# Turning tiles on TensorE in the type of the rounded halves, through second names over the same bytes

## What is computed

```python
x = x + xattn(layernorm(x), ctx, ctx, mask, wq, wk, wv, wo)   # x, ctx: (8, 512, 512)
x = x + ffn(layernorm(x), Wr, Wg, Wu, Wd, Sg, Su, Sd, expert_bias)

# xattn: H = 16 heads of 32, KVH = 2 heads of K and V
scores = einsum('bhqd,bhkd->bhqk', rope(Q), rope(K)) / sqrt(32)
out = einsum('bhqk,bhkd->bhqd', softmax(where(mask == 0, -1e9, scores)), V) @ wo
# ffn: 8 experts of width 256, two per token, beside a shared one of width 512
h = silu(gate) * up
out = sum over the two experts of weight * (h @ Wd) + silu(xf @ Sg) * (xf @ Su) @ Sd
```

## Time and profile before

| | |
|---|---|
| time of three runs, us | 1424.04, 1426.14, 1426.20; median 1426.14 |
| span of the profiled execution, us | 1422.9 (it has no other time of its own) |
| TensorE busy | 1373.1 us (97%) |
| weight loads (PEld) busy | 1067.2 us (75%) |
| VectorE busy | 960.4 us (67%) |
| ScalarE busy | 844.9 us (59%) |
| GpSimd busy | 581.4 us (41%) |
| chain that ended last | TensorE 82%, VectorE 6%, ScalarE 4% |

### The profile page before, as it was taken

The page is one execution under the profiler, slowest core; times in us unless marked ns, Lnnn a source line. Parts: engine busy times, 40 slices in busy tenths (PEclk is TensorE's granted clock), DMA queues, the critical chain, the costliest instruction groups (busy, mean ns, idle before and its releaser), DMA issues.

```text
span 1422.9 us, 28293 instructions
## 1 busy us (share of the span) xinstructions
PE 1373.1 (97%) x8110; PEld 1067.2 (75%) x8110; DVE 960.4 (67%) x2655; ACT 844.9 (59%) x1951; POOL 581.4 (41%) x724
## 2 busy tenths in 40 slices
PE   6898999999999999999898999999999999999997
PEld 4675777877777777777576777777777888888885
DVE  6888888888888888988777666666653334333342
ACT  2788979889798897988983222222213434444342
POOL 4443523435244343342253432333334555555553
PEclk9899999999999999999999999999999999999999
DMA  5545464564645646445465222222257779785542
GB/s 203 152 145 146 135 190 139 152 185 137 188 136 149 187 131 190 142 140 157 114 202 203 85 87 90 82 75 84 73 140 205 201 178 260 204 197 103 111 76 37
DMA packets 146070, 206.62 MB, mean 145 GB/s; under 512 B 35456, under 2 KB 73088, under 8 KB 145923
## 3 DMA queue, kind: packets, MB, share of 16 engines
q1 hardware_dynamic: 124562, 166.91, 38.1%
q0 software_dynamic: 17952, 33.64, 12.3%
q10 hardware_dynamic: 3408, 4.26, 0.9%
HBM read 105.49 MB, written 69.35 MB: 123 GB/s over the span
## 4 chain that ended last, share of the span: by engine, by line
PE 82%; DVE 6%; ACT 4%; issue 3%; DMA 2%; SPq 1%; POOL 1%; DVEq 0%; POOLq 0%; ACTq 0%
PE psum L693 13%; PE psum L1494 13%; PE psum L1496 12%; PE psum L1495 12%; PE psum L808 7%; PE psum L787 7%; PE psum L738 3%; PE psum L739 3%; PE psum L740 3%; ACT a_probs L591 2%; PE psum L1561 2%; PE psum L708 2%; DVE a_probs L955 1%; ACT a_probsT L597 1%; PE psum L1590 1%
## 5 line engine op out<-in xcount | busy, mean ns | idle before, releaser
L591 ACT ACTIVATE a_probs<-a_probs,a_low 128x512 f32<-128x512 f32 x512 | 366.6, 716 | 83.7 <-DVE a_low L955 82.2
L955 DVE CUSTOM_DVE_ANT_0 a_probs<-psum,a_bias 128x512 f32<-128x512 f32 x512 | 345.4, 685 | 76.5 <-PE psum L787 73.2
L693 PE MATMUL psum<-a_ident,a_probs 128*128 128x128 f32 x2048 | 311.0, 274 | 7.8 <-ACT a_probsT L597 5.9
L693 PEld LDWEIGHTS psum<-a_ident,a_probs 128*128 128x128 f32 x2048 | 245.3, 141 | 77.0 <-issue 25.6
L787 PE MATMUL psum<-a_kT,a_q_stack 128*128 128x512 f32 x512 | 247.2, 484 | 10.1 <-DVE a_low L955 5.4
L597 ACT ACTIVATE a_probsT<-psum 128x512 f32<-128x512 f32 x328 | 190.7, 582 | 10.0 <-PE psum L693 10.0
L1363 POOL DMA_INDIRECT out<-b_y,b_pairs_sb x71 | 112.6, 1586 | 148.7 <-DMA out<-b_y,b_pairs_sb 85.9
L1795 DVE SCALAR_TENSOR_TENSOR b_v_hidden<-b_v_hidden,psum 128x256 f32<-128x256 f32 x71 | 29.9, 421 | 165.9 <-ACT b_v_hidden L1459 165.9
L961 DVE COPY a_probsT<-psum 128x512 f32<-128x512 f32 x184 | 126.0, 685 | 6.1 <-PE psum L693 4.2
L1494 PE MATMUL psum<-b_w,b_vT_hi 128*128 x284 | 117.4, 413 | 0.1
L808 PE MATMUL psum<-a_probsT,a_v 128*32 128x512 f32 x1024 | 116.7, 595 | 0.0
(11 more groups left out here) (218 smaller groups left out, 3054.3 us busy)
## 6 DMA issues: line engine op xcount, KB each, us to landing
b_w<-w_halves SPq DMA_DIRECT2D x16, 1536.0 KB
a_q_stack<-a_qT_hi SPq DMA_DIRECT2D x254, 64.0 KB, 2.0
a_q_stack<-a_qT_lo SPq DMA_DIRECT2D x253, 64.0 KB, 2.0
w_halves<-a_w_hi SPq DMA_DIRECT2D x96, 128.0 KB, 2.0
w_halves<-a_w_lo SPq DMA_DIRECT2D x96, 128.0 KB, 1.9
a_xT_in<-in_x_turned SPq DMA_DIRECT2D x32, 256.0 KB, 2.9
a_ctx_in<-in_ctx SPq DMA_DIRECT2D x32, 256.0 KB, 3.0
a_x_in<-in_x SPq DMA_DIRECT2D x32, 256.0 KB, 3.2
```

The source lines that it names most:

```text
L591: nc.scalar.activation(probs[:, h % 2, t], probs[:, h % 2, t], ACT.Exp, bias=low[:, h % H, t:t + 1], scale=-1.0, accum_out=total[:, h // G ...
L693: last = nc.tensor.transpose(out[:, P * i:P * (i + 1)], src(i), identity[:])
L955: nc.vector.tensor_tensor_reduce(probs[:, h % 2, t], psum[:, t % 2], bias[:, t], 1.0, HUGE, ALU.add, ALU.min, low[:, h % H, t:t + 1]).then ...
```

## The change

The turns of probabilities, Q, normalised rows, gathered rows and hidden tiles are asked for in `F32R`. For each of those tiles a second tensor is allocated over the same bytes with the type `F32R` (`bits`), the output in PSUM is named in that type by `bitcast`, and the moving operand is `ident_r`. The two identities swap their places in memory, so that `ident_r` is the one that stays through the feed-forward. Each engine has as many instructions as before, in the same order.

```diff
-    "rope_q": 94208, "rope_k": 95232, "ident_r": 96256, "pick_raw": 96768, "pick": 97280, "probsT": 98304, "bias": 139264, "kT": 147456,
+    "rope_q": 94208, "rope_k": 95232, "ident_r": 207872, "pick_raw": 96768, "pick": 97280, "probsT": 98304, "bias": 139264, "kT": 147456,
...
-    "wkv": 205824, "ident": 207872, "k_cos": 208384, "k_sin": 208640, "k_rot": 208896, "low": 209152, "total": 209408, "inverse": 209664,
+    "wkv": 205824, "ident": 96256, "k_cos": 208384, "k_sin": 208640, "k_rot": 208896, "low": 209152, "total": 209408, "inverse": 209664,
...
+    def bits(name, shape):
+
+        return nc.alloc_sbuf_tensor_at(f"a_{name}_bits", shape, F32R, offset=base + ATTENTION_PLACES[name])
...
+    probs_bits = bits("probs", [P, 2, TT, L])
+    q_bits = bits("q", [P, 2, TT, D])
...
-        def four(out, src, identity):
+        def four(out, src):
             for i in range(4):
-                last = nc.tensor.transpose(out[:, P * i:P * (i + 1)], src(i), identity[:])
+                last = nc.tensor.transpose(out[:, P * i:P * (i + 1)].bitcast(F32R), src(i), ident_r[:])
             return last
...
-            four(in_ring(part, b, "qT", i), lambda t: q[:, batch, t, P * g:P * (g + 1)], ident).then_inc(s["qT_filled"], 1)
+            four(in_ring(part, b, "qT", i), lambda t: q_bits[:, batch, t, P * g:P * (g + 1)]).then_inc(s["qT_filled"], 1)
...
-            four(out, lambda c: probs[:, h % 2, t, P * c:P * (c + 1)], ident).then_inc(s["t_filled"], 1)
+            four(out, lambda c: probs_bits[:, h % 2, t, P * c:P * (c + 1)]).then_inc(s["t_filled"], 1)
...
+    xn_bits, rows_bits, v_hidden_bits = bits("xn", [P, XN_SLOTS, D]), bits("rows", [P, X_SLOTS, D]), bits("v_hidden", [P, 2, F])
...
-                last = nc.tensor.transpose(psum[:, XT + n % 2, P * c:P * (c + 1)], xn[:, n % XN_SLOTS, P * c:P * (c + 1)], ident[:])
+                last = nc.tensor.transpose(psum[:, XT + n % 2, P * c:P * (c + 1)].bitcast(F32R), xn_bits[:, n % XN_SLOTS, P * c:P * (c + 1)], ident_r[:])
...
-                last = nc.tensor.transpose(psum[:, XT + n % 2, P * c:P * (c + 1)], rows[:, n % X_SLOTS, P * c:P * (c + 1)], ident[:])
+                last = nc.tensor.transpose(psum[:, XT + n % 2, P * c:P * (c + 1)].bitcast(F32R), rows_bits[:, n % X_SLOTS, P * c:P * (c + 1)], ident_r[:])
...
-                mm = nc.tensor.transpose(psum[:, HT + n % 2, P * i:P * (i + 1)], v_hidden[:, n % 2, i:F:FC], ident[:])
+                mm = nc.tensor.transpose(psum[:, HT + n % 2, P * i:P * (i + 1)].bitcast(F32R), v_hidden_bits[:, n % 2, i:F:FC], ident_r[:])
```

More of the change, by code:

```diff
@@ L1076, in on_vector @@
         bodies(dve, body)
-    shared = dict(s, ident=ident, half=half, stored=stored, stacked=stacked)
+    shared = dict(s, ident_r=ident_r, half=half, stored=stored, stacked=stacked)
     return shared, on_sync, on_gpsimd, on_scalar, on_tensor, on_vector
 def ffn_phase(nc, ctx, psum, attention, k, x2_rows, xn_rows, out_rows, xn_all, out_all, wr, sg, su, sd, expert_bias, pairs, halves, tile_table):
+    tile_at = {}
     where = [(nc.sbuf_base + 31) // 32 * 32]
@@ L1092, in put, with bits @@
             where[0] = (at + size + 31) // 32 * 32
+        tile_at[name] = at
         return nc.alloc_sbuf_tensor_at("b_" + name, shape, dt, offset=at)
+    def bits(name, shape):
+        return nc.alloc_sbuf_tensor_at(f"b_{name}_bits", shape, F32R, offset=tile_at[name])
     def sem(name):
@@ L1121, in ffn_phase @@
     pairs_sb = put("pairs_sb", [P, VISITS, 2], I32)
-    ident, half = attention["ident"], attention["half"]
+    ident_r, half = attention["ident_r"], attention["half"]
     tri, ones = put("tri", [P, P], at=constants), put("ones", [P, P], at=constants + 512)
```

## The result

The changed kernel takes 1415.06 us (median of 4 runs, 1409.39 to 1415.83), the kernel before 1426.02 on the same chip (4 runs). The ratio is 0.9918, with a 95% interval of 0.9900 to 0.9936. That is 11 us less, where 36 were forecast, and 10 us above the top of the range. The profiled execution has a span of 1414.0 us, 8.9 less than before, and a mean granted clock of 0.985 (before 0.994).

A forecast was written before the change was run, and what follows sets the result against it. TensorE was taken to bound every stage, with VectorE and ScalarE close behind in the attention. 29 us there plus 7 in the feed-forward made 36, from 1426.1 to 1390 us; range 1350 to 1405 us.

The forecast's parts named there:

- What a rounded turn costs: All rounded turns: the load sets the pace at 0.085 us against 0.109, saving 0.07 us a group of four.
- The first rival: All rounded turns: the load hides as well, a turn costs 0.06 us, kernel at 1351 us; chance 0.17.
- the second, that nothing changes: All rounded turns: loads go at the ordinary 0.11 us or the type has no effect, 1426 us; chance 0.08.
- I take the middle of 21 and 38, 29 us: Attention: gain between 21 us, limited by other engines' idle time, and 38 us, with TensorE the bound everywhere.
- its own sign of being wrong: Attention: the prediction is wrong if this gives less than 21 us though turns have the forecast pace.
- The least of 2.6 us a batch: Attention: eight windows' gains, each capped by idle time of the busier of VectorE and ScalarE; 21 us over eight batches.
- The reason for going above the least: Attention: four banks and six steps of scores let TensorE run ahead and spend its lead later; up to 38 us.
- The low end of the range, 1376 us: Whole kernel: fastest end of the forecast, from turn distances of 0.08 to 0.09 and 21 to 38 us for the attention.
- third rival: Attention: shorter passes make TensorE look idle, the clock drops to half, kernel ends slower at 1442 us; chance 0.05.
- What is late next: Attention: once turns are shorter, ScalarE's exp and VectorE's add and minimum are late; no size given.
- 103 x 0.07 = 7 us: Feed-forward: groups of normalised and gathered rows each gain 0.07 us, all of it on the path.
- I count 0, with 0 and 71 x 0.07 = 5 us as ends: Expert visits: the 71 pairs of hidden tiles gain nothing, as their load sets the pace already; at most 5 us.

The follow-up runs named there:

- first12_only: The kernel before, with rounded turns in the first 12 attention steps of the first batch alone: 1428.01 us, ratio 1.0009.
- the K tile ahead: The changed kernel with GpSimd making a batch's second K tile ahead of the sixth weight piece: 1411.43 us, repeated at 1413.22 us.
- the repeats: Side by side: changed kernel again, 1416.95 us; with K tile before weight piece, 1413.22; that plus float32 turns where the clock fell, 1407.26.
- mixed: The changed kernel with float32 turns in attention steps where TensorE was seen to wait or the clock to fall: 1412.79 us, ratio 0.9904.

## Why the prediction was wrong, point by point

**What a rounded turn costs** was right: 0.085 forecast, 0.082 to 0.088 between most loads measured, 0.46 us for four against 0.48, and 0.60 us for a step. "Each turn is a weight load of the data and a pass of the identity", and with the rounded type the load sets the pace. The first rival, a hidden load at 0.06, has fallen, and so has the second, that nothing changes. The edits costed at nothing cost nothing.

**The attention is the step that failed.** The prediction put it: "I take the middle of 21 and 38, 29 us". The profiled execution gives 747.0 - 742.5 = 4.5 us up to the last step. That is also less than the 21 us which the prediction had named as its own sign of being wrong. Two things are wrong in that line.

The first is the bound below. The least of 2.6 us a batch was read from windows of eight steps that begin at a batch's first step. So the last window, where ScalarE is full, and the first, where all have room, are counted apart, as if the first could take its own 0.56. In truth it pays for the last one: what ScalarE has left over is waited for behind the border of the batch, in a step that lasts 1.18 us, and this window gives 0.21 us less than nothing. The third and the fifth window, which have room too, give 0.20 and 0.26 us in place of 0.56, so idle time of the other engines, taken over eight steps, is no measure of what a window can give. An undisturbed batch gives 1.3 to 2.3 us. The reason for going above the least, that "TensorE can run ahead through a full window and spend it in the next", is true of the running ahead and wrong of the spending. Here a lead over ScalarE was no gain, since ScalarE had to catch up before the next batch. With the copies halved, five of the eight windows of batch 5 lose 0.6 us each and a sixth 0.5; the fourth and the fifth do not, so the copies were most of what was in the way and not all. The low end of the range, 1376 us, does not follow from its terms either: at 0.08 us a turn, 647 groups x 0.087 = 56 us give 1370. This part is 29 - 8 x 2.1 = 12 us of the 27 that the profiled execution falls short.

The second is that all eight batches were counted alike. Four of them (0, 1, 3 and 7) went by -0.2, +1.0, +1.0 and +1.5 us where -2.1 was to be had, which is 12 us more. They hold all of the added half clock and, batch 7 apart, 3.2 of the 4.5 us of waits for K tiles. The **third rival**, the clock, had a chance of 0.05 in the form of a kernel that ends slower, and that form did not occur. But it needs no such form to cost. Its own test, a clock below 1.00 between 46 and 1360 us, came out positive, and the kernel lost in part by it: 0.8 us in place of a gain at the start of the attention, shown by first12_only. Taking it away in the attention, with the K tile ahead, brings the median from 1413.22 to 1407.26 us, but the two profiles differ by 0.9 us there, so these 6 us are not shown to be the clock's. It should have been a term of the sum in every case and not a case by itself. Its evidence against was a mean ("under 5% in all"), and the mean did not tell: the clock fell behind single stretches such as the one with 1.56 of 3.40 us above.

Of the waits forecast, those for ScalarE and for VectorE's minimum came. "What is late next" left out GpSimd's K tile. It had 0.9 us of waits before, and stood in its row of work behind a piece of weights that waits for a DMA and an addition to Q.

**Feed-forward.** "103 x 0.07 = 7 us" and nothing for the pairs; 4.4 measured. The rows' term was right (0.07 a group). Of the pairs the prediction said "I count 0, with 0 and 71 x 0.07 = 5 us as ends", and they lie beyond these ends: they cost 0.02 to 0.03 x 71, some 1.4 to 2.1 us. "Their load sets the pace already" was right. What failed is the silent premise that this load is the same in both types, though rows 5 showed the contrary for loads in one piece, 0.06 in float32 and 0.08 rounded.

The Trainium skill (TensorE: Matmul & The Clock Gate, Part 4: PE-mode transpose) says of turns that they do not count as busy in the same way for the clock. The runs disagree. With float32 turns in the first steps the clock rises at 44 to 47 us (seven profiles, the kernel before among them), with rounded ones the last such stretch ends at 52.4 to 55.7 us (nine, with 52.8 in the changed kernel and in first12_only), and between the kernel before and first12_only nothing but these turns differs. The page's rule would have left the clock as it was, and so have supported the forecast; the measurement decides.

The shortfall of the profiled execution is 36 - 8.9 = 27 us, and these three make it: 12 us in the undisturbed pace, 12 in the four disturbed batches, 2.6 in the feed-forward. This is the sum of one execution; in the second profile of the same kernel the attention is 2 us shorter and the rest 2 us longer. How those second 12 divide between clock and K tile stays open. The medians of the repeats give 6 us to the clock and 3.7 to the K tile, the attention steps of their profiles 1 and 8. Also open is what sets the two long waits for VectorE in the kernel with halved copies. The hidden tiles in float32 with all others rounded were not tried, because the identities of both types don't stay in memory through the feed-forward.

## What to carry to other kernels

Price a cheaper instruction by the distance of starts, weight load and following load included, and then ask of each loop where the lead of the quickened engine ends. If the engine behind it is full for any part of the loop, read the windows across the loop's border too, because here the lead was given back there.

A shorter turn on TensorE can cost its clock where it waits anyway: twelve of them did so in first12_only. Keeping the old form where it waits cost nothing (mixed, with a third of its groups unchanged), so take the cheap form where TensorE is the bound and try the old one elsewhere. When an engine gets quicker, list what feeds it from an engine with other work in its row, waits for DMAs included, for a piece of work that was just in time before is late then.

## What the runs showed of the hardware that was not expected

What type the turns have moves TensorE's clock. Twelve groups of rounded turns in place of float32 ones are enough for a second stretch of 3.4 us at 1.2 GHz, behind 3.4 us in which TensorE was busy for 1.56 in place of 2.25, and for 16 steps that take 0.8 us longer instead of 0.8 shorter.

The load of a tile to be turned is 0.03 us slower in the rounded type than in float32, in one piece (0.06 and 0.085 from start to start) and when every second element is read (0.11 and 0.14). In one piece this costs nothing, since a float32 turn takes 0.109 from start to start anyway. For the strided tiles, whose load already set the pace, the change of type is a loss, of 0.02 to 0.03 us a pair.
